# Three block transposes a batch at steps 5, 13 and 21 instead of 5, 8 and 12, and the low half of the context rows made by VectorE instead of GpSimd

## What is computed

```python
q = (text_hidden @ Wq).reshape(B, T_text, 16, 128).transpose(0, 2, 1, 3)
k = (vision_tokens @ Wk).reshape(B, T_vis, 8, 128).transpose(0, 2, 1, 3)     # T_vis = 1500
v = (vision_tokens @ Wv).reshape(B, T_vis, 8, 128).transpose(0, 2, 1, 3)
scores = jnp.einsum('bhtd,bhsd->bhts', q, k) / scale
attn = jax.nn.softmax(jnp.where(mask, scores, -jnp.inf), axis=-1)
out = jnp.einsum('bhts,bhsd->bhtd', attn, v)
return out.transpose(0, 2, 1, 3).reshape(B, T_text, 2048) @ Wo
```

## Time and profile before

| | before |
|---|---|
| median of 2 runs | 1952.93 (1952.05 and 1953.82) |
| profiled execution, its own time | 1952.05 |
| its span, first to last instruction | 1950.2 |
| granted TensorE clock, mean | 0.930 of full speed |
| TensorE matmul busy | 1661.2, 85% of the span |
| VectorE busy | 1199.1, 61% |
| ScalarE busy | 1033.4, 53% |
| GpSimd busy | 946.3, 49% |

### The profile page before, as it was taken

The page is one execution under the profiler, slowest core; times in us unless marked ns, Lnnn a source line. Parts: engine busy times, 40 slices in busy tenths (PEclk is TensorE's granted clock), DMA queues, the critical chain, the costliest instruction groups (busy, mean ns, idle before and its releaser), DMA issues.

```text
span 1950.2 us, 26771 instructions
## 1 busy us (share of the span) xinstructions
PE 1661.2 (85%) x8882; PEld 1431.6 (73%) x8882; DVE 1199.1 (61%) x3102; ACT 1033.4 (53%) x1780; POOL 946.3 (49%) x790
## 2 busy tenths in 40 slices
PE   8999788787979797878797878797988897869896
PEld 7988677676767676767676767676767676758896
DVE  5556665666666666666666666566666666547447
ACT  5443465655555555555555556555555555434452
POOL 1210354555555555555555555555555555344635
PEclk9999899999989898989898989898999898989999
DMA  4335866666666666666666666666676665533333
GB/s 174 114 129 181 197 162 154 162 154 160 157 158 157 160 158 158 156 162 158 159 152 157 155 153 157 152 157 152 157 153 157 152 158 124 135 127 105 102 97 101
DMA packets 171973, 291.22 MB, mean 149 GB/s; under 512 B 44702, under 2 KB 138560, under 8 KB 171712
## 3 DMA queue, kind: packets, MB, share of 16 engines
q1 hardware_dynamic: 129904, 266.49, 53.3%
q10 hardware_dynamic: 38912, 14.80, 3.2%
q0 software_dynamic: 3024, 8.26, 1.6%
HBM read 189.11 MB, written 100.38 MB: 148 GB/s over the span
## 4 chain that ended last, share of the span: by engine, by line
DMA 28%; PE 19%; POOL 14%; DVE 11%; issue 7%; ACT 6%; SPq 4%; ACTq 0%; DVEq 0%; POOLq 0%
DMA p_store<-b_by_block 26%; POOL b_keyed_over L1247 9%; POOL b_c_raw_over L1235 4%; DVE b_by_block L1093 3%; SPq L796 3%; DVE b_pT_lo L1098 2%; ACT b_p L975 2%; DVE b_p L1072 2%; PE b_turn L882 2%; PE b_score L868 2%; PE b_score L870 2%; PE b_score L869 2%; PE b_out L916 2%; PE c_gate L1647 2%; ACT b_pT_hi L961 2%
## 5 line engine op out<-in xcount | busy, mean ns | idle before, releaser
L1072 DVE CUSTOM_DVE_ANT_0 b_p<-b_score,b_mask_add 128x500 f32<-128x500 f32 x672 | 450.5, 671 | 358.4 <-PE b_score L870 237.3
L1247 POOL TENSOR_TENSOR b_keyed_over<-b_keyed,b_pT_hi 125x384 fp32r<-125x384 f32 x372 | 367.8, 1010 | 481.4 <-ACT b_pT_hi L968 480.9
L961 ACT CAST b_pT_hi<-b_turn 125x512 fp32r<-125x512 f32 x384 | 224.1, 585 | 366.4 <-PE b_turn L882 346.7
L900 PE MATMUL b_out<-b_pT_hi,b_c_hi 125*128 125x512 f32 x384 | 193.5, 504 | 208.8 <-DVE b_pT_lo L1098 208.7
L975 ACT ACTIVATE b_p<-b_p,b_shift 128x1500 f32<-128x1500 f32 x224 | 347.2, 1550 | 24.6 <-DVE b_top_min L1081 24.6
L968 ACT CAST b_pT_hi<-b_keyed 125x384 fp32r<-125x384 f32 x384 | 187.4, 507 | 234.3 <-PE b_out L902 121.8
L1098 DVE TENSOR_TENSOR b_pT_lo<-b_turn,b_pT_hi 125x512 fp32r<-125x512 f32 x384 | 264.0, 688 | 61.5 <-ACT b_pT_hi L961 61.0
L868 PE MATMUL b_score<-b_cT_hi,b_q_hi 128*128 128x500 f32 x672 | 275.3, 410 | 9.3 <-issue 7.5
L869 PE MATMUL b_score<-b_cT_lo,b_q_hi 128*128 128x500 f32 x672 | 272.1, 405 | 0.0
L870 PE MATMUL b_score<-b_cT_hi,b_q_lo 128*128 128x500 f32 x672 | 270.7, 403 | 0.0
L1093 DVE STREAM_TRANSPOSE b_by_block<-b_p 128x1536 f32<-128x1536 f32 x96 | 170.1, 1771 | 132.4 <-DMA p_store<-b_by_block 132.4
(11 more groups left out here) (261 smaller groups left out, 3242.0 us busy)
## 6 DMA issues: line engine op xcount, KB each, us to landing
p_store<-b_by_block SPq DMA_DIRECT2D x384, 192.0 KB, 8.8
b_keyed<-p_store SPq DMA_DIRECT2D x96, 768.0 KB, 14.5
cT_in<-in_ctxT SPq DMA_DIRECT2D x32, 750.0 KB, 7.0
b_c_raw<-in_ctx SPq DMA_DIRECT2D x32, 750.0 KB
q_store<-a_fold_in_or_q_stage SPq DMA_DIRECT2D x16, 896.0 KB, 4.2
q_in<-q_store SPq DMA_DIRECT2D x32, 448.0 KB, 17.9
b_rden_all<-rden_store ACTq DMA_DIRECT2D x32, 256.0 KB, 8.7
b_rden_all<-rden_store ACTq DMA_DIRECT2D x32, 192.0 KB, 6.5
```

What stands on the lines that cost most here:

```text
L900: pe.matmul(out, hi, pT_hi[:, c % 3, 0:w], start=(c == 0), stop=False)
L961: act.copy(pT_hi[:, c % 3, 0:w], turn_bank[c % 3][0:CK, 0:w]).then_inc(hi_done, 1)
L1072: dve.tensor_tensor_reduce(out=row(m, u)[:, keys], in0=score_bank[j][:, 0:FW], in1=mask_add[:, b, keys], scale=1.0, scalar=-3.0e38, op0=AL ...
L1247: pool.tensor_tensor(keyed_chunk(keyed_lo, c), keyed_chunk(keyed, c), by_blocks(pT_hi[:, c % 3, 0:128 * EVEN]).bitcast(F32), ALU.subtract) ...
```

## The change

The block transposes of the even units move from steps 5, 8 and 12 to steps 5, 13 and 21. The third store of a batch moves behind the loads of transposed context, mask, and the norm's store and residual in the SP queue. `c_rest` moves from GpSimd to VectorE, one piece at each of steps 17, 18 and 19 behind the step's other work, in batch 0 too, where the cast of the context rows now also stands at step 15 and not behind the last step.

```diff
-        BLOCKS_AT = (5, 8, 12)
+        BLOCKS_AT = (5, 13, 21)
...
-        C_PARTS = 3
+        C_LO_AT = range(17, 20)
+        C_PARTS = len(C_LO_AT)
...
                 if m:
                     store_p(m, 1)
-                store_p(m, 2)
                 if m + 2 < B:
                     load_cT(m + 2)
                     load_mask(m + 2)
                 if m % 2 and m >= 3:
                     store((m - 3) // 2)
                     residual((m - 1) // 2)
+                store_p(m, 2)
...
-                    if n == C_HI_AT and m:
+                    if n == C_HI_AT:
                         c_round(m)
                 if m == 0:
                     cT_round(1)
-                    c_round(0)
...
+            def c_rest(m, part):
+                b, cols = m % 2, slice(part * CH * CD // C_PARTS, (part + 1) * CH * CD // C_PARTS)
+                if part == 0:
+                    dve.wait_ge(c_hi_done, m + 1)
+                dve.tensor_tensor(c_lo[b][:, cols], c_raw[b][:, cols], c_hi[b][:, cols].bitcast(F32), ALU.subtract).then_inc(
+                    c_lo_done, 1)
...
             def block_step(m, n):
                 if n in BLOCKS_AT:
                     turn_blocks(m, BLOCKS_AT.index(n))
+                if n in C_LO_AT:
+                    c_rest(m, C_LO_AT.index(n))
...
-                if m == 0:
-                    for part in range(C_PARTS):
-                        c_rest(0, part)
-                else:
+                if m:
                     for c in range(CH):
                         keyed_rest(m - 1, c)
                         if c == 1 and m % 2 and m >= 3:
                             rstd((m - 3) // 2)
-                        if c % 3 == 2 and c // 3 < C_PARTS:
-                            c_rest(m, c // 3)
```

More of the change, by code:

```diff
@@ L1229, in cT_rest @@
                 pool.tensor_tensor(cT_lo[b][:], cT_in[:], cT_hi[b][:].bitcast(F32), ALU.subtract).then_inc(cT_lo_done, 1)
-            def c_rest(m, part):
-                b, cols = m % 2, slice(part * CH * CD // C_PARTS, (part + 1) * CH * CD // C_PARTS)
-                if part == 0:
-                    pool.wait_ge(c_hi_done, m + 1)
-                pool.tensor_tensor(c_lo[b][:, cols], c_raw[b][:, cols], c_hi[b][:, cols].bitcast(F32), ALU.subtract).then_inc(
-                    c_lo_done, 1)
             def oT_rest(m):
```

## The result

The changed kernel takes 1836.38 us (median of 1843.36 and 1829.39) against 1952.93: 0.940 of it, with an interval of 0.925 to 0.956. With more runs, in a second session (experiment 1), it was 1827.06 against 1955.83, 0.933 (0.931 to 0.936). Its runs lie further apart than those of the kernel before: 1822 to 1841 there, where before lay within 1953 to 1958. Forecast were 1838 us and a range of 1785 to 1900. The profiled execution took 1843.36, with a span of 1841.5 and a mean granted clock of 0.982.

The account below looks back on a forecast made before the run. It took the bound to be VectorE's 132.4 us wait for p_store stores, which makes TensorE wait for the odd rows' low part. 15 plain batches at 5.5 and 14 others at 2.3 give 114 us: 1838, range 1785 to 1900.

Parts of the forecast that it names:

- Plain batch, 5.5 forecast: The 15 batches without projection matmuls: context rows are late next, each batch gets 5.5 us shorter.
- 7.5: Plain batch: TensorE gets the third keyed chunk at 965.6 and not 973.14, 7.5 us earlier.
- 1.7 for a slow stretch: Plain batch: TensorE's clock runs low again after its remaining wait, costing 1.7 us.
- 1.0 for collisions: Plain batch: c_rest on VectorE and GpSimd's keyed_rest hold each other up, charged 1.0 us a batch.
- wait of some 3.7 us: Plain batch: TensorE still waits some 3.7 us for the third keyed chunk, behind the late context cast.
- rival 1: The new waits are smaller: clock may stay high, c_rest may fit GpSimd's gaps; 1776, or 1807 for half; chance 0.14.
- Projecting batch, 2.3 forecast: The other 14 batches, with projection matmuls at steps 9 to 12: VectorE is late next, gain 2.3 us each.
- the 4.18: Projecting batch: TensorE's idle time at the last p_rest, 4.18 us, should go with VectorE's wait.
- VectorE is late next: Projecting batch: transposes and c_rest delay the last unit's scores; the first turn comes only 3.1 us earlier.
- I charge nothing: SP's queue: the third store, directly ahead of the keyed loads, may delay them but costs 0 us.
- rival 2: The third unit's store holds the keyed and context loads on SP: 74 us given back, 1912; chance 0.17.
- rival 3: SP's wait ahead of the third keyed load, at the slowest landing, 18.6 us: slower, 2157; chance 0.05.

Follow-up runs that it names:

- experiment 1: The changed kernel run again unaltered in a second session, against the kernel before: 1827.06 us, 0.933.
- experiment 10: The kernel before with only the reciprocals' store changed, to 128 writes of 128 bytes after a VectorE block transpose: 1795.8 us, 0.918 of the kernel before.
- experiment 9: The complete changed kernel with the reciprocals transposed in blocks on VectorE and stored as 128 writes of 128 bytes: 1771.13 us, 0.905 of the kernel before.
- experiment 12: The changed kernel with the reciprocals stored as 128 writes of 128 bytes, but the context rows' low half left on GpSimd: 1770.5 us, 0.906.
- experiment 4: The changed kernel with the three c_rest pieces on VectorE cut from 512 to 8 columns, products taking the high half instead: 1850.22 us, 0.945.
- experiment 2: The kernel before with the turns at 5, 13 and 21 and the third store moved, c_rest staying on GpSimd: 1837.32 us, 0.938.
- experiment 6: The changed kernel with the load into cT_in ahead of the second unit's stores on SP: 1821.37 us, 0.9315 of the kernel before.
- experiment 3: The changed kernel with turns back at 5, 8 and 12 and SP's old order, c_rest staying on VectorE: 1940.09 us, 0.992.
- experiment 7: The changed kernel with the third unit's stores back in their old place, ahead of the load into cT_in: 2007.85 us, 1.026.
- experiment 5: The changed kernel with each reciprocals' store as 128 writes of 12 or 16 bytes, leaving the reciprocals in the wrong order: 1759.81 us, 0.900.

## Why the prediction was right, and where it was not

**The wait that goes.** "The 132.4 us of VectorE's wait should go, and with them TensorE's 9.76 and 4.18": right. For this it was enough to follow where the stores and transposes stand. But why those stores landed late was never asked. The prediction takes the 10.2 us at the median as given (and as the stores' own, which is 8.8), sees that "only 28 GB/s move" over 938 to 948, and uses this as a comfort for loads issued late. Experiment 10, where 0.6 us of it are left, shows that the form of the reciprocals' store was the cause of the 132.4. The change moves the turns out of the way of a symptom: 108.7 us of span. Taking away the cause is worth 158 us (experiment 10), and the change on top of it 25 more (experiment 9 against 10: 1795.8 less 1771.1). These 25 are what the transposes at 8 and 12 cost by being where they are: TensorE's 70.3 fall to 17.1, its wait for GpSimd grows from 36.5 to 55.6, and with the turns alone moved (experiment 12) the time is the same.

**Plain batch, 5.5 forecast, 6.8 measured.** Its terms were 7.5, less 1.7 for a slow stretch, plus 0.7 for GpSimd, less 1.0 for collisions. The first half became 7.5 us shorter, and that this equals the first term is luck: at the median it is 8.2 shorter (19.6 us), and one batch of 27.2, in which ScalarE waits 9.5 for the reciprocals' store, brings the mean down. The second half became 0.7 longer. The term that failed is the 1.7, and behind it the "wait of some 3.7 us" that was to bring it: ScalarE's wait for the context rows is 15.9 us in 11 pieces of at most 3.0, not near 50, and no wait of TensorE for GpSimd is longer than 2.7. The first half of a plain batch, 982.20 to 1001.80, runs at full clock (2.4 GHz), where before the clock was at its lower level (1.2 GHz, 0.50) for 3.4 us:

```profile
982.20:1001.80 19.60, 18.49 (x96) 15.13 (x96) 15.87 (x41) 12.41 (x20) 9.97 (x5) 1.00 0.88 204
```

The mean clock went to 0.982, not to 0.95. This is rival 1's mechanism, half of it: the clock stays high, but the collisions are there. By the prediction's own sign ("if the 3.7 us wait isn't there (rival 1)") its account of the plain batch is wrong, though the range holds.

**Projecting batch, 2.3 forecast, 0.7 measured.** By halves, the forecast takes 4.18 and more off the first and gives 1.9 back in the second (4.18 less 2.3). Measured are 2.6 off the first and 1.9 back in the second. So the term that was mis-sized is the 4.18: TensorE's wait for the low part in that half falls from 4.0 to 1.1 us a batch, and not to nothing; in experiment 9 it is 0.55, and the half is 3.5 shorter. The 1.9 came out in size, but the step behind it, "VectorE is late next", is not borne out. VectorE is busy, and ScalarE waits for its shifts (99.4 us against 25 before), but this is not what TensorE ends up waiting for: with hardly any `c_rest` (experiment 4) or with all of it on GpSimd (experiment 2) that half takes 21.3 and 21.5 us instead of 21.7, and the changed kernel itself took 21.5 in experiment 1. Turns hardly wait for exponentials either: that row has 0.4 us in one piece, though the last exponentials now end 0.6 us before the first turn on average, where it was 2.5. TensorE waits 2.2 us a batch for GpSimd's rests, about five times, and 0.7 for the first chunks of the next batch. The 0.7 are gone in experiment 9, and in experiment 6 that half is 20.7 us: they belong to `cT_in`. Below stand ScalarE's cast of it in one projecting batch, its idle time in brackets, and then SP's issue of that load:

```profile
1066.97 1.45 ACT L1004 CAST b_cT_hi<-cT_in 128x1500 fp32r<-128x1500 f32 x1 [2.21 <-DMA cT_in<-in_ctxT]
```

```profile
1053.31 1.00 SPq L779 DMA_DIRECT2D cT_in<-in_ctxT  x1
```

From its issue to the cast that waits for it are 13.7 us, and the store of the reciprocals was issued at 1052.34, just ahead of it. The 2.2 us behind GpSimd remain in experiment 9 (2.24) and in experiment 12 (2.33), so they are neither the transfers' nor due to where `c_rest` stands. Experiments 10 and 12 differ only in the steps of the turns and the place of the third store, and that half takes 19.2 us in the one and 20.9 in the other. This is as much as the first half gains (26.1 to 24.4): where no transfer is late, the move brings a projecting batch nothing and a plain one 1.5. So the lateness comes with the turns' new place. By which path it reaches TensorE, VectorE's transposes or ScalarE's queue, stays open.

**`c_rest` on VectorE.** Forecast were a mean between 0.65 and 1.2, collisions included, and `keyed_rest` above 1.01; measured are 1.07 and 1.10. Both are right. In one batch of the changed kernel all three pieces fall on GpSimd's work. The first two are held, and the third takes what a piece takes while GpSimd idles (0.68 to 0.69, 4 of the 96), but then it is GpSimd whose rest takes 1.78 instead of 1.00 (timelines of VectorE and of GpSimd):

```profile
1053.60 1.33 DVE L1112 TENSOR_TENSOR b_c_raw_over<-b_c_raw,b_c_hi 125x512 fp32r<-125x512 f32 x1
...
1055.45 1.42 DVE L1112 TENSOR_TENSOR b_c_raw_over<-b_c_raw,b_c_hi 125x512 fp32r<-125x512 f32 x1
...
1057.92 0.68 DVE L1112 TENSOR_TENSOR b_c_raw_over<-b_c_raw,b_c_hi 125x512 fp32r<-125x512 f32 x1
```

```profile
1057.70 1.78 POOL L1249 TENSOR_TENSOR b_keyed_over<-b_keyed,b_pT_hi 125x384 fp32r<-125x384 f32 x1
```

The Trainium skill, GPSIMD Engine Reference, section Specifications, says the two share SBUF interfaces for such instructions, and experiment 12 agrees: what GpSimd is spared (124) the pair pays in full (113 and 33), and the move is worth nothing. GpSimd's relief, 0.7 a batch, was 0.5 where VectorE had time to spare (experiment 3).

**SP's queue, "I charge nothing".** For the third store this held, though it does hold the keyed loads, as rival 2 says. In the changed kernel and then in experiment 9, waits of SP:

```profile
SPq L806 <- DMA p_store<-b_by_block: 183.1, 28, 12.0
```

```profile
SPq L808 <- DMA p_store<-b_by_block: 2.0, 2, 1.2
```

The rule cited there (the Trainium skill, DMA: Bandwidth & Descriptors, section Queues, rings and completion order) has a semaphore's increment wait for the earlier writes of the same DMA engine, those of other queues too. The 183.1 us that become 2.0 when the reciprocals' writes are few agree with it, but slower writes without any such order would show the same. That this cost so little fits the argument against rival 2, "loads issued in this stretch gain nothing by being early": ScalarE has no row for the keyed loads, and 15.9 us for the context rows. No run tests it by itself. What the step overlooked is the load into `cT_in`: it stands behind the second unit's stores, which moved from step 8 to 13. It was on SP's list, and the prediction followed the third store only. Its price is seen where it is larger, in experiment 7: the same load behind the third store, and the change is a loss of 2.6%. So a loss by one place on SP, rival 3's kind, was there to be had, but not in rival 3's place.

**In sum.** The forecast named the mechanism of the gain: VectorE's wait goes, TensorE's with it. That the size came out within 2 us of the first median (11 us above the second session's 1827.06) is in good part luck, with 1.3 a plain batch too little and 1.6 a projecting batch too much (1.6 and 1.1 by experiment 1). One bound is added up wrongly: a whole `keyed_rest` for each piece is 14 x 3 x 0.51 + 15 x (3.03 - 1.0) = 52 us over what is charged, not about 40. The one expectation that should have been doubted most, TensorE's wait at L900 under 20 us, was 69.0: transfers that are late for the small writes' sake. It is 17.1 in experiment 9.

## What to carry to other kernels

Where an engine waits for a transfer, look at the GB/s of the windows ahead of it before moving the work that waits: busy DMA engines that move little may point, as here, to a store of many tiny pieces, perhaps of another queue and of a few KB only. Make such a store contiguous first (a small block transpose on chip cost 0.21 us), and only then tune the order. After a step is moved, follow every load that stands behind its DMA in the same queue to the step that wants it, and compare the two distances. Work that goes from GpSimd to VectorE with both operands in SBUF should be priced for the pair.

## What the runs showed of the hardware

- A store of 384 or 512 separate 4-byte values, 1.5 or 2 KB, held the loads of the other queue for about ten us: 28 GB/s against 292 in the same stretch, a keyed load under way for 14.5 us at the median against 5.9, and 158 of 1954 us over 64 such stores, 2.5 us for each. As 128 writes of 12 to 16 bytes (experiment 5) or of 128 bytes (experiments 9 and 10) it did no such harm. Whether the number of the writes or their 4 bytes each does it, the runs don't separate. The Trainium skill, DMA: Bandwidth & Descriptors, section Rules for kernel authors, has a strided last dimension become a descriptor for each element and tells one to rearrange it. The runs agree; that the harm falls on other queues' loads is what they add.
- The row of the tile rden_store doesn't give it away: 7.5 us at the median before and 7.0 in experiment 10. It holds the landings of the loads of the reciprocals alone; those of the narrow stores aren't recorded.
- Less work on an engine can make a kernel slower: experiment 4 lost 23 us with some 0.5 us a piece less for VectorE to do.
- Two subtractions with their operands in SBUF, on VectorE and GpSimd: on VectorE 0.68 us alone and 1.33 or 1.42 together, or else 0.68 there and 1.78 instead of 1.00 on GpSimd; one of only 8 columns took 0.15 at the shortest and 0.99 at the longest, the latter about one whole rest of GpSimd (1.01). These durations fit the two running one after the other, as the earlier trace rows suggested.
